# The fifth tap of a composed filter: its low part beside its high part in one stationary operand, two products with two further tables in place of three products

## What is computed

```
x = x + s4(cond(x, style, weights1...))     # x: 64 batches, 64 channels, 1024 positions
x = x + ffn(cond(x, style, weights2...))
```

```
s = style @ mw.T + mb
weight = SCALE * w * s[:, None, :, None]
demod = rsqrt(sum(weight * weight) + EPS)
out = conv(x, weight * demod) + b          # and blur before or behind, by the layer
```

## Time and profile before

| what | us |
|---|---|
| median of 3 runs | 1339.88 (1339.38 to 1341.36) |
| the profiled execution, its own time | 1337.98 |
| its span, first to last instruction | 1336.1 |
| PE busy, share of the span | 1293.9 (97%) |
| PEld busy | 1226.3 (92%) |
| DVE busy | 1044.7 (78%) |
| ACT, POOL busy | 798.9 (60%), 806.3 (60%) |
| mean granted clock of TensorE, 1 is full speed | 0.995 |

### The profile page before, as it was taken

One profiled execution on the slowest core, in us unless ns is written; L12 is line 12 of the kernel. 1 busy time (PEld: TensorE's weight loads), 2 busy tenths in 40 slices (PEclk: granted clock), 3 DMA queues, 4 the chain that ended last, 5 costly groups with the idle time before them and its releaser, 6 DMA issues.

```text
span 1336.1 us, 22883 instructions
## 1 busy us (share of the span) xinstructions
PE 1293.9 (97%) x8127; PEld 1226.3 (92%) x8127; DVE 1044.7 (78%) x2442; ACT 798.9 (60%) x1625; POOL 806.3 (60%) x611
## 2 busy tenths in 40 slices
PE   3789999999999999999999999999999999999998
PEld 3589899899899999899999999999999999999998
DVE  7878878778877778778778888787878878787873
ACT  4587787778777787775445544545554554545440
POOL 6468887666676677664555545555555555555542
PEclk9899999999999999999999999999999999999999
DMA  3234444444455654452542523425243342524322
GB/s 129 77 105 134 133 133 133 133 132 133 132 140 148 155 150 141 126 160 79 119 117 85 147 77 103 130 77 151 81 123 109 95 136 78 151 80 120 111 84 88
DMA packets 86274, 158.20 MB, mean 118 GB/s; under 512 B 26633, under 2 KB 48402, under 8 KB 86034
## 3 DMA queue, kind: packets, MB, share of 16 engines
q1 hardware_dynamic: 84898, 154.79, 41.5%
q10 hardware_dynamic: 1264, 1.96, 0.5%
HBM read 93.79 MB, written 33.56 MB: 95 GB/s over the span
## 4 chain that ended last, share of the span: by engine, by line
PE 86%; DVE 5%; POOL 4%; ACT 2%; issue 1%; DMA 1%; SPq 0%; DVEq 0%; POOLq 0%; ACTq 0%
PE psum L1770 28%; PE psum L1772 27%; PE psum L1771 27%; PE psum L1884 2%; POOL xs_l L931 1%; DVE psum L1544 1%; DMA w3T<-in_w_dram 1%; POOL vs_l L926 0%; POOL vbuf L910 0%; POOL vbuf L906 0%; PE psum L283 0%; DVE y_l L1490 0%; POOL vbuf L908 0%; DVE a_l L1520 0%; DVE a_f L1525 0%
## 5 line engine op out<-in xcount | busy, mean ns | idle before, releaser
L1770 PE MATMUL psum<-wt_h,u_h 128*128 128x386 f32 (+1 forms) x760 | 260.9, 343 | 0.0
L1772 PE MATMUL psum<-wt_h,u_l 128*128 128x386 f32 (+1 forms) x760 | 257.9, 339 | 0.0
L1771 PE MATMUL psum<-wt_l,u_h 128*128 128x386 f32 (+1 forms) x760 | 257.6, 339 | 0.0
L1544 DVE STREAM_TRANSPOSE psum<-vbuf 32x256 f32<-32x256 f32 x480 | 218.8, 456 | 11.8 <-ACT vbuf L1137 0.7
L1520 DVE SCALAR_TENSOR_TENSOR a_l<-psum,tabs,a_h 128x512 fp32r<-128x512 f32 x128 | 95.9, 751 | 158.7 <-ACT a_h L1119 158.6
L906 POOL TENSOR_TENSOR vbuf<-vbuf 128x512 f32<-128x512 f32 x64 | 97.1, 1518 | 190.7 <-ACT vbuf L1151 190.7
L920 POOL TENSOR_TENSOR vm_f<-vm_f 128x512 f32<-128x512 f32 x64 | 82.7, 1292 | 177.5 <-DVE vm_l L1514 177.1
L1144 ACT ACTIVATE vbuf<-psum,tabs 128x512 f32<-128x512 f32 x128 | 105.2, 822 | 117.4 <-PE psum L1772 113.5
L1770 PE MATMUL psum<-a_h,vm_h 128*128 128x256 f32 x512 | 148.2, 289 | 3.2 <-ACT vbuf L1144 3.0
L1771 PE MATMUL psum<-a_l,vm_h 128*128 128x256 f32 x512 | 145.7, 285 | 0.0
L1770 PEld LDWEIGHTS psum<-wt_h,u_h 128*128 128x128 f32 x760 | 143.5, 189 | 2.2
(11 more groups left out here) (309 smaller groups left out, 3803.7 us busy)
## 6 DMA issues: line engine op xcount, KB each, us to landing
vm_f<-vv SPq DMA_DIRECT2D x256, 112.0 KB, 4.5
xin<-in_x_ph_dram SPq DMA_DIRECT2D x32, 512.0 KB, 5.0
xr<-in_x_row_dram SPq DMA_DIRECT2D x32, 512.0 KB, 4.2
x1d<-xr SPq DMA_DIRECT2D x64, 256.0 KB, 3.3
xin<-x1d SPq DMA_DIRECT2D x32, 512.0 KB, 5.4
xr<-x1d SPq DMA_DIRECT2D x64, 256.0 KB, 5.9
xo<-in_b_base_dram SPq DMA_DIRECT2D x32, 512.0 KB, 5.9
out_dram<-xo SPq DMA_DIRECT2D x31, 512.0 KB, 2.9
```

The source lines that it names most:

```text
L1544: ins = V.transpose(ps_x[to, :, :].rearrange("p b (k n) -> p b k n", n=P)[:, :, :, frm], v3[frm, :, :].rearrange("p b (k n) -> p b k n", n ...
L1770: nc.tensor.matmul(to, stat_h, mov_h, start=first_ and n == 0, stop=False, skip_group_check=True)
L1771: nc.tensor.matmul(to, stat_h, mov_l, start=False, stop=False, skip_group_check=True)
L1772: ins = nc.tensor.matmul(to, stat_l, mov_h, start=False, stop=end, skip_group_check=True)
```

## The change

For n = 2 step 2 now takes one stationary operand that holds both parts of the fifth tap: the high part in the lower half of the partitions, the low part in the upper half, which was zero. Two tables are added: rt_h has the lower half of r_h in both halves, rt_l the lower half of r_l below and zero above. One product with each gives the same three partial sums. Nothing else of the result changes.

- PE: `step2` has eight products for a tile in place of nine; it waits for the new tables at the first tile of each stage.
- DVE: `composed1` makes for each batch a low part of two blocks (128 x 128) in place of three (128 x 192), and a further instruction (64 x 64) that writes the fifth tap's low part into the upper half of c1_h. Four instructions in place of two.
- ACT: `fifth_high`, two copies of 64 x 320, behind `r_high` in the start, and at the end of turn 30. POOL: `fifth_low`, one copy of 64 x 320 with a wait before and behind it, behind `r_low` in the start, and in turn 30; a memset at the start.
- For space the row of zeros `zero` now lies in vv, so that the first `composed_out` waits for the DMA that reads it.

```
@@ program
-    c1_l = sb("c1_l", [P, 3, 2, C], FR)
+    c1_l = sb("c1_l", [P, 2, 2, C], FR)
...
+    zero = vv[0:1, 0:PAD // C, :].rearrange("p k c -> p (k c)")
@@ gpsimd
             ins.then_inc(pads_ready, 1)
             pool.wait_ge(pads_ready, 1)
+            G.memset(rt_l[HIGH, :, :].bitcast(F32), 0.0).then_inc(pads_ready, 1)
+            pool.wait_ge(pads_ready, 2)
...
+            def fifth_low(c):
+                pool.wait_ge(r_lo, c + 1)
+                if c:
+                    pool.wait_ge(step2_done, at(TILES - 1))
+                    pool.wait_ge(v3_val, at(TILES - 2))
+                G.tensor_copy(rt_l[LOW, :, :], r_l[LOW, c, :, :].bitcast(F32)).then_inc(rt_lo, 1)
+                pool.wait_ge(rt_lo, c + 1)
...
             r_low(0)
+            fifth_low(0)
...
+                if turn_is(i, TILES - 2):
+                    fifth_low(1)
@@ scalar
+            def fifth_high(c):
+                act.wait_ge(r_hi, c + 1)
+                if c:
+                    act.wait_ge(step2_done, at(TILES - 1))
+                for half in HALF:
+                    ins = A(rt_h[half, :, :], r_h[LOW, c, :, :].bitcast(F32), ACT.Copy)
+                ins.then_inc(rt_hi, 1)
...
             r_high(0)
+            fifth_high(0)
...
                     composed1(i + 2)
+                if turn_is(i, TILES - 2):
+                    fifth_high(1)
@@ vector, composed1
                 for b in range(2):
-                    ins = V.scalar_tensor_tensor(out=c1_l[:, :, b, :], in0=ps_taps[:, :, b, :],
-                                                 scalar=tabs[:, c, T_S3, batch(t, b)], in1=c1_h[:, :, b, :].bitcast(F32),
+                    V.scalar_tensor_tensor(out=c1_l[:, :, b, :], in0=ps_taps[:, 0:2, b, :],
+                                           scalar=tabs[:, c, T_S3, batch(t, b)], in1=c1_h[:, 0:2, b, :].bitcast(F32),
+                                           op0=ALU.mult, op1=ALU.subtract)
+
+                    ins = V.scalar_tensor_tensor(out=c1_h[HIGH, 2, b, :], in0=ps_taps[LOW, 2, b, :],
+                                                 scalar=tabs[LOW, c, T_S3, batch(t, b)], in1=c1_h[LOW, 2, b, :].bitcast(F32),
                                                  op0=ALU.mult, op1=ALU.subtract)
                 ins.then_inc(c1_lo, 1)
@@ vector, composed_out
+                if g == 0:
+
+                    ve.wait_ge(k_out, 16)
@@ tensor, step2
                 if g in (0, TILES):
-                    pe.wait_ge(r_lo, c + 1)
+                    pe.wait_ge(rt_lo, c + 1)
+                    pe.wait_ge(rt_hi, c + 1)
                 pe.wait_ge(c1_lo, at(g))
-                for n in range(3):
-                    ins = product(ps_step[:, C * n:C * (n + TAPS)],
-                                  [(c1_h[:, n, :, :].rearrange("p b o -> p (b o)"), c1_l[:, n, :, :].rearrange("p b o -> p (b o)"),
-                                    r_h[:, c, :, :].rearrange("p d o -> p (d o)"), r_l[:, c, :, :].rearrange("p d o -> p (d o)"))],
-                                  n == 0, n == 2)
+                for n in range(2):
+                    product(ps_step[:, C * n:C * (n + TAPS)],
+                            [(c1_h[:, n, :, :].rearrange("p b o -> p (b o)"), c1_l[:, n, :, :].rearrange("p b o -> p (b o)"),
+                              r_h[:, c, :, :].rearrange("p d o -> p (d o)"), r_l[:, c, :, :].rearrange("p d o -> p (d o)"))],
+                            n == 0, False)
+
+                for r in (rt_h, rt_l):
+                    ins = nc.tensor.matmul(ps_step[:, C * 2:C * (2 + TAPS)], c1_h[:, 2, :, :].rearrange("p b o -> p (b o)"),
+                                           r[:, :, :].rearrange("p d o -> p (d o)"), start=False, stop=r is rt_l,
+                                           skip_group_check=True)
                 ins.then_inc(step2_done, 1)
```

More of the change, by code:

```diff
@@ L167, in build @@
         sh.r_l = sb("r_l", [P, 2, TAPS, C], FR)
+        sh.rt_h = sb("rt_h", [P, TAPS, C], FR)
+        sh.rt_l = sb("rt_l", [P, TAPS, C], FR)
         sh.x1w = sb("x1w", [P, 2, 2, C])
@@ L407, in program @@
     tabs, iota8, vec = sh.tabs, sh.iota8, sh.vec
-    r_h, r_l, x1w = sh.r_h, sh.r_l, sh.x1w
+    r_h, r_l, rt_h, rt_l, x1w = sh.r_h, sh.r_l, sh.rt_h, sh.rt_l, sh.x1w
     bt_h, bt_l, toep_h, toep_l = sh.bt_h, sh.bt_l, sh.toep_h, sh.toep_l
@@ L485, in program @@
         warm = tb("warm", [1, 1])
-        zero = tb("zero", [1, PAD])
         flip = tb("flip", [P, P])
@@ L527, in program @@
     style_in, style1_in, wT_in, wT1_in = sem("style_in"), sem("style1_in"), sem("wT_in"), sem("wT1_in")
-    r_terms, r_sum, r_hi, r_lo = sem("r_terms"), sem("r_sum"), sem("r_hi"), sem("r_lo")
+    r_terms, r_sum, r_hi, r_lo, rt_hi, rt_lo = (sem("r_terms"), sem("r_sum"), sem("r_hi"), sem("r_lo"),
+                                                   sem("rt_hi"), sem("rt_lo"))
     w3_in, cm_in, cm1_in, m0_in = sem("w3_in"), sem("cm_in"), sem("cm1_in"), sem("m0_in")
@@ L706, in loads @@
                 sp.wait_ge(zero_set, 1)
-                sp.dma_start(sh.kpad[0:1, 0:PAD], zero[:, :]).then_inc(k_out, 16)
+                sp.dma_start(sh.kpad[0:1, 0:PAD], zero).then_inc(k_out, 16)
             def later_loads():
@@ L820, in _ @@
             G = nc.gpsimd
-            G.memset(zero[:, :], 0.0).then_inc(zero_set, 1)
+            G.memset(zero, 0.0).then_inc(zero_set, 1)
             G.memset(flat4(sh.xe), 0.0)
@@ L1945, in edges_read @@
                     pe.wait_ge(var_ready, 2)
-            pe.wait_ge(pads_ready, 1)
+            pe.wait_ge(pads_ready, 2)
             def first_turns():
```

## The result

The changed kernel takes **1362.34 us** (median of 4 runs, 1360.96 to 1365.47), the kernel before 1339.63 beside it: ratio 1.0174, 95% interval 1.0162 to 1.0186. The forecast was 1341.9 with a range to 1346. The change costs some 23 us, eleven times what was forecast. Stage 2 loses, as forecast, but five times as much; stage 1 was to gain and loses.

What follows compares the result with a forecast made beforehand. PE's busy time was taken as the bound, with little slack at the evacuation and lora's operand. Start +0.9, stage 1 -1.9 and stage 2 +3.0 gave +2.0 us, a median of 1341.9 us, range 1337.4 to 1346.

Steps and rivals of the forecast that it cites:

- Part 1: Product removed from step2 on PE: plain turns gain 0.135 us each in stage 1, 0.074 in stage 2.
- The two lateness places: PE's step2 against ACT's evacuation, -0.15 us in stage 1, -0.09 in stage 2; lora's operand in stage 2, -0.09.
- the formulas for their cost: On PE, a lateness D costs about D + 0.02 us at the evacuation and D - 0.02 at lora's operand.
- Part 2: Instructions added on DVE: +0.27 us a turn; stage 2 +5.1, stage 1 +0.2, start +0.53.
- two instructions of 0.13 us: The two added DVE instructions in `composed1` cost only their fixed part, together +0.27 us for each turn.
- The fixed part: Size-independent time of a DVE subtraction in `composed1`, about 0.13 us of 0.33; ends 0.08 and 0.28.
- four late turns: Stage 2 turns where lora's operand is already late, so they pay all of the added DVE time, +1.07 us.
- the fifth: Stage 2 turn with lora's operand at +0.01 us lateness, to pay 0.26 us.
- Its own sign of being wrong: On DVE, `composed1`'s four instructions taking 1.2 us, where 0.93 us would show the forecast right.
- The rival "don't overlap": Added DVE instructions each wait for the one before: +0.50 us a turn, total 1349.5 us; chance 0.12.
- c_l was to stay hidden: In stage 1, c_l on DVE still ends before PE's last product ahead of step2, lateness -0.04 to -0.21 us.
- 0.53 on DVE's path: In the start DVE sets the pace; c_l of tiles 0 and 1 lies on its path: +0.53 us.

Runs made afterwards that it cites:

- nothing added: The changed kernel without the two added VectorE instructions, the fifth tap's low part left out of the result: 1332.26 us, ratio 0.9947.
- the crossing alone: The kernel before, nine products, its two subtractions cut into four, the 64x64 ones written to the upper partitions: 1366.85 us; kept on the lower half: 1344.99 us.
- grouping: The changed kernel with the two 128x128 subtractions first and the two 64x64 ones behind them: 1353.99 us, ratio 1.0107.
- `res` first: The changed kernel with the two resolvent products ahead of tile 1's `composed1` in the opening: 1361.20 us, ratio 1.0158.
- lora first: The changed kernel with lora's operand made ahead of `composed1` on DVE in stage 2: 1349.83 us, ratio 1.0086.
- the split on 128: The kernel before, nine products, its two 128x192 subtractions cut into four, 128x128 and 128x64 in turn, all on 128 partitions: 1346.54 us, ratio 1.0050.
- three changes of order: The changed kernel with 64x64 subtractions grouped last, lora's operand ahead of `composed1` in stage 2, and `res` ahead of tile 1's `composed1`: 1338.67 us, ratio 1.0002.
- the copy: The changed kernel with the old two 128x192 subtractions and one 64x128 DVE copy to the upper half instead of four subtractions: 1390.25 us, ratio 1.0372.

## Why the prediction was wrong

**Part 1 held.** With nothing added stage 2 is 23.33 us a turn, 0.07 shorter (forecast 0.074), and the plain turns of stage 1 give 0.15 (0.135). The two lateness places and the formulas for their cost were right: in the changed kernel the evacuation is 0.05 late and puts the next product back by 0.06 (formula 0.07), lora's operand is 0.60 late and puts its second product back by 0.58 (formula 0.58). One slip of bookkeeping is without effect: the turns that part 1 names are 55 of its 61.

**Part 2 failed, in the term "two instructions of 0.13 us".** The fixed part was read well: four instructions in one place take 0.91 us, +0.25, against the forecast 0.27. What was missed is that the added ones write to the upper half and their neighbours to the lower, four changes of 0.105 us each. With 0.67 in place of 0.27 the working of the prediction gives for stage 2: 24 turns of (-0.09 + 0.67 - 0.02) = 0.56, 13.4; four late turns +2.7; the fifth +0.7; less 2.1: +14.7, against +15.7 measured. So this one term is the miss of stage 2. Its own sign of being wrong, four instructions in 1.2 us, came true with 1.33. The rival "don't overlap" had the mechanism, and even named the other half, with 0.12; its +0.50 was too small, since it took 0.74 for the old pair, which is its time to the end, not to the next start (0.66), and left out the gaps between the four. And the argument against it, that neighbours of this kind overlap by 0.07, came from neighbours that all stay in one place. The rule that would have decided it stands in the section named above of the Trainium skill; the prediction drew on another one.

**Stage 1** was forecast at -1.9 and came to +5.9. c_l was to stay hidden at -0.04 to -0.21. In plain turns it is late by 0.08, again by the 0.67 in place of 0.27, and step2's second product comes 0.25 behind the first in place of 0.15:

```profile
453.65 0.42 PE L1806 MATMUL psum<-r_h,c_h 128*128 128x320 f32 x1
453.91 0.31 PE L1807 MATMUL psum<-r_l,c_h 128*128 128x320 f32 x1
```

That leaves 0.05 of the 0.15 gained. The rest of the loss comes in single turns, by 0.3 to 1.1 us each. That the same term is behind it is shown by the table (the crossing alone makes 7.0 us in stage 1, grouping takes back 3.3); by which path it reaches the worst of these turns stays open, as said above. Turn 30's copies cost 0.5, as forecast.

**The opening** was forecast at +0.9. y_l did slip in between POOL's instructions (it ended at 21.40 in place of 24.14), and tile 0's step2 came 2.0 us earlier, where the prediction had c_l start as before. But the term "0.53 on DVE's path" left out what is next on DVE: `res`, which missed its place ahead of POOL's xs_l and took 1.7 us more. With `res` first 1.0 of the +2.7 is taken back; where the other 1.7 comes from was not separated. Part of it may be scatter: lora first, whose opening has the same code, stands at +3.2, and the split on 128, in which nothing crosses, at +2.5.

## What to carry to other kernels

Price a small VectorE instruction by where it writes and not by its size alone: each change of the output's first partition against the neighbour ended an overlap and cost 0.105 us here, so instructions that write to the same place belong together. Before adding to a chain that has 0.1 us to spare, look on the same engine for work that has microseconds to spare, and put that behind the chain's: here three changes of order decided over 23 us. And an edit that moves a VectorE instruction without a PSUM operand by half a microsecond can put it behind a long GpSimd instruction, as it did here with `res`, and the copy met such an instruction in 63 of 64 places; look at what starts next to it.

## What was not expected of the hardware

- Of two neighbours among `composed1`'s instructions on DVE the second starts 0.07 to 0.08 us before the first ends if both write to the same first partition, and 0.015 to 0.03 behind its end if not; 64 partitions or 128 make no difference (0.91 us for either).
- A 64x128 copy within SBUF took 0.22 us alone and up to 2.95 beside POOL, and ended 0.08 to 0.09 behind a POOL instruction in 63 of 64 cases. A 128x512 product with both inputs in SBUF took 2.37 in place of 0.68. `composed1`'s other instructions, which have an operand in PSUM, kept their times.
